# Two expert layers with the second product's weight held stationary and the rows turned back a block later

## The reference

```python
# layer 0: each row goes to one of 8 experts (arg max of the gate)
h = gelu(rows @ W1[e] + b1[e])          # 128 -> 512
f = h @ W2[e] + b2[e]                   # 512 -> 128
# layer 1: each row goes to its two best experts, each with a limited number of places
h = gelu(rows @ W1[e] + b1[e]);  ye = h @ W2[e] + b2[e]
f = ye[first] * w1 + ye[second] * w2
```

## Time and profile before

| | us |
|---|---|
| median of 3 runs | 1137.81 |
| the profiled execution, its time | 1137.35 |
| its span | 1135.5 |
| TensorE busy in the span | 1012.4 (89%) |
| expert stage, layer 0 (second products, first to last start) | 340.2 to 424.5 |
| expert stage, layer 1 | 945.7 to 1093.1 |

### The profile page before, as it was taken

One profiled execution on the slowest core, in us unless ns is written; L12 is line 12 of the kernel. 1 busy time (PEld: TensorE's weight loads), 2 busy tenths in 40 slices (PEclk: granted clock), 3 DMA queues, 4 the chain that ended last, 5 costly groups with the idle time before them and its releaser, 6 DMA issues.

```text
span 1135.5 us, 22426 instructions
## 1 busy us (share of the span) xinstructions
PE 1012.4 (89%) x6668; PEld 745.6 (66%) x6668; DVE 686.7 (60%) x2553; ACT 659.4 (58%) x1973; POOL 668.5 (59%) x821
## 2 busy tenths in 40 slices
PE   5798999999999999899999998998889978999950
PEld 2675566666668996566666665666568857989840
DVE  6737876776763336776776777867654353345326
ACT  4635667667755557667666666675554434544434
POOL 3425588788854555677676687887345422545443
PEclk9678999999999999999999999999999889999985
DMA  9200112202526742203302122032131044777745
GB/s 293 63 5 1 26 37 63 68 24 64 151 47 197 221 147 62 55 25 70 64 7 60 28 57 65 25 76 53 31 83 29 29 140 142 211 209 224 216 134 149
DMA packets 97385, 103.70 MB, mean 91 GB/s; under 512 B 10447, under 2 KB 85238, under 8 KB 97040
## 3 DMA queue, kind: packets, MB, share of 16 engines
q1 hardware_dynamic: 90256, 89.96, 30.2%
q0 software_dynamic: 7040, 12.66, 3.2%
HBM read 77.29 MB, written 25.28 MB: 90 GB/s over the span
## 4 chain that ended last, share of the span: by engine, by line
PE 55%; DVE 14%; issue 12%; ACT 8%; POOL 4%; DMA 3%; SPq 2%; another core or an unknown queue 1%; POOLq 0%; DVEq 0%; ACTq 0%
PE bank L1138 11%; PE bank L641 8%; PE bank L630 8%; PE bank L1167 7%; PE bank L1194 5%; PE bank L1182 4%; PE bank L1157 4%; DVE arena L1731 4%; PE bank L1219 3%; ACT arena L1479 3%; POOL arena L906 2%; DVE arena L1740 2%; ACT arena L1468 1%; PE bank L1071 1%; ACT XN L355 1%
## 5 line engine op out<-in xcount | busy, mean ns | idle before, releaser
L1479 ACT ACTIVATE arena<-arena 128x128 f32<-128x128 f32 (+1 forms) x512 | 226.9, 446 | 118.9 <-DVE arena L1731 118.4
L1731 DVE CUSTOM_DVE_ANT_0 arena<-bank,arena 128x128 f32<-128x128 f32 (+1 forms) x512 | 182.9, 413 | 141.1 <-PE bank L1167 134.8
L906 POOL TENSOR_TENSOR arena<-arena 128x512 f32<-128x512 f32 x128 | 132.7, 1042 | 164.4 <-ACT arena L1455 157.0
L1138 PE MATMUL bank<-arena 128*128 128x512 f32 x384 | 210.3, 637 | 15.5 <-ACT arena L1468 11.7
L1740 DVE COPY arena<-bank 128x384 f32<-128x384 f32 x256 | 130.3, 549 | 24.3 <-PE bank L1182 20.3
L604 POOL DMA_INDIRECT expert_out<-arena x78 | 77.0, 987 | 101.6 <-DVE arena L710 86.1
L921 POOL TENSOR_TENSOR arena<-arena 128x512 f32<-128x512 f32 x128 | 129.9, 1049 | 1.3
L1182 PEld LDWEIGHTS bank<-const,arena 128*128 128x128 f32 x768 | 91.7, 142 | 56.2 <-issue 56.0
L1455 ACT ACTIVATE arena<-bank 128x512 f32<-128x512 f32 x192 | 112.6, 587 | 26.9 <-PE bank L1138 26.7
L1167 PE MATMUL bank<-arena 64*128 64x128 f32 (+1 forms) x1024 | 120.0, 353 | 8.4 <-DVE arena L1731 5.5
L1194 PE MATMUL bank<-arena 128*64 128x256 f32 (+1 forms) x1024 | 111.8, 339 | 6.9 <-DVE arena L1740 6.3
(11 more groups left out here) (277 smaller groups left out, 1806.1 us busy)
## 6 DMA issues: line engine op xcount, KB each, us to landing
arena<-in_wp SPq DMA_DIRECT2D x39, 514.0 KB
arena<-recip_rows SPq DMA_DIRECT2D x30, 512.0 KB, 6.2
XN<-in_wp SPq DMA_DIRECT2D x23, 514.0 KB
arena<-expert_rows SPq DMA_DIRECT2D x62, 129.0 KB
arena<-expert_out SPq DMA_DIRECT2D x16, 256.0 KB, 5.4
arena<-in_b SPq DMA_DIRECT2D x62, 64.0 KB
expert_out<-fill SPq DMA_DIRECT2D x11, 338.6 KB, 7.6
expert_rows<-fill SPq DMA_DIRECT2D x1, 2967.0 KB, 22.5
```

The lines of the kernel that those rows point to most:

```text
L906: pool.tensor_tensor(sq[:, i % 2], r, r, ALU.mult).then_inc(S["sq_done"], 1)
L1138: mm = pe.matmul(RING[bnk][:, :], xa[:, p, t * P:(t + 1) * P], wqkv[:, 512 * k:512 * k + 512], start=True, stop=True)
L1479: ins = act.activation(w, w, ACT.Exp, bias=nm[:, p, 16 * t + h:16 * t + h + 1], scale=-1.0, accum_out=den[:, p, 16 * t + h:16 * t + h + 1])
L1731: ins = v.tensor_tensor_reduce(out=SPb[:, c % 2, 384 * k + P * t:384 * k + P * t + n], in0=SBANK[k][:, P * t:P * t + n], in1=alibi[:, h, N ...
```

## The change

The second product is turned round: W2's block is now the stationary operand and 256 columns of hidden values move, so its result has the 128 features on the partitions and the 256 rows as columns. The bias b2 is then one number per partition: it is loaded as a column of 128 partitions x 1, and ScalarE adds it as it takes the product out of PSUM (`biased`, into the new buffer `yT`). Layer 0's tanh and product work on `yT`. Since the rows must be sent as rows, TensorE transposes the two halves back (`back`), in the step of the next block between `up` and `down`, and VectorE copies them out (`rows_out`) ahead of its `evac_x`. GpSimd sends after that copy in both layers. SyncE reloads weights after `yT_evac`. After the last block each stream has one more `biased`, `back` and `rows_out`.

```diff
@@ ffn_sync
-                sp.dma_start(b2b[:, q], B2[bass.ds(e, 1)].to_broadcast([P, D])).then_inc(S[f"w_in{q}"], 16)
+                sp.dma_start(b2c[:, q:q + 1], B2[bass.ds(e, 1)].rearrange("e d -> d e")).then_inc(S[f"w_in{q}"], 16)
...
-                sp.wait_ge(S["ye_evac"], j + (base + 1))
+                sp.wait_ge(S["yT_evac"], j + (base + 1))
@@ ffn_send
-                pool.wait_ge(S["ye_evac" if layer else "y_ready"], j + (base + 1))
+                pool.wait_ge(S["ye_evac"], j + (base + 1))
@@ ffn_tensor, down and the new back
+                for c in range(FC):
+                    mm = pe.matmul(YB[p][:, 0:BLK], wb[:, q, DFF + c * D:DFF + (c + 1) * D], hT[:, p, c * BLK:(c + 1) * BLK],
+                                   start=(c == 0), stop=(c == FC - 1))
+                mm.then_inc(S["ye_full"], 1)
+
+            def back(j, q):
+
+                pe.wait_ge(S["yT_evac" if layer else "y_ready"], j + ((base if layer else 0) + 1))
                 for t in range(2):
-                    for c in range(FC):
-                        mm = pe.matmul(YB[p][:, t * D:(t + 1) * D], hT[:, p, c * BLK + t * P:c * BLK + (t + 1) * P],
-                                       wb[:, q, DFF + c * D:DFF + (c + 1) * D], start=(c == 0), stop=(c == FC - 1))
-                mm.then_inc(S["ye_full"], 1)
+                    mm = pe.transpose(YB[q % 2][:, BLK + t * D:BLK + (t + 1) * D], yT[:, q % 2, t * P:(t + 1) * P], ident)
+                mm.then_inc(S["y_turned"], 1)
@@ step
                     up(j + 1, (q + 1) % NBUF, i + (q + 1) // NBUF)
+                if not isinstance(j, int) or j:
+                    back(j - 1, (q + NBUF - 1) % NBUF)
                 down(j, q)
...
+            back(nblk - 1, (nblk - 1) % NBUF)
@@ ffn_scalar
-            def half_tanh(j, q, first=False):
-
-                act.wait_ge(S["ye_evac"], j + 1)
-                if not first:
-                    act.wait_ge(S["y_ready"], j - 1)
-                act.activation(th[:, q % 2, :], yb[:, q, :], ACT.Tanh, scale=0.5).then_inc(S["tanh_done"], 1)
+            def biased(j, q, first=False):
+                act.wait_ge(S["ye_full"], j + (base + 1))
+                if base or not first:
+                    act.wait_ge(S["y_turned"], j + (base - 1))
+                act.activation(yT[:, q % 2, :], bank[6 + q % 2][:, 0:BLK], ACT.Identity, bias=b2c[:, q:q + 1], scale=1.0)\
+                   .then_inc(S["yT_evac"], 1)
+                if not layer:
+
+                    act.wait_ge(S["yT_evac"], j + 1)
+                    act.activation(th[:, q % 2, :], yT[:, q % 2, :], ACT.Tanh, scale=0.5).then_inc(S["tanh_done"], 1)
 
             def both(j, q, i):
                 gelu(j, q, i)
-                half_tanh(j - 1, (q + NBUF - 1) % NBUF)
-
-            if layer:
-                quads(act, 0, nblk - 1, gelu)
-            else:
-                gelu(0, 0, 0)
-                for j in range(1, NBUF):
-                    gelu(j, j, 0)
-                    half_tanh(j - 1, j - 1, j < 3)
-                quads(act, NBUF, nblk - 1, both)
-                half_tanh(nblk - 1, (nblk - 1) % NBUF)
+                biased(j - 1, (q + NBUF - 1) % NBUF)
+
+            gelu(0, 0, 0)
+            for j in range(1, NBUF):
+                gelu(j, j, 0)
+                biased(j - 1, j - 1, j < 3)
+            quads(act, NBUF, nblk - 1, both)
+            biased(nblk - 1, (nblk - 1) % NBUF)
@@ ffn_vector
-            def add_b2(j, q, i):
-                v.wait_ge(S["ye_full"], j + (base + 1))
-                v.wait_ge(S[f"w_in{q}"], (i + (counts[q] + 1)) * 32)
-                v.tensor_tensor(yb[:, q, :].rearrange("p (t d) -> p t d", t=2),
-                                YB[q % 2][:, 0:2 * D].rearrange("p (t d) -> p t d", t=2),
-                                b2b[:, q].unsqueeze(1).to_broadcast([P, 2, D]), ALU.add).then_inc(S["ye_evac"], 1)
+            def rows_out(j, q):
+                v.wait_ge(S["y_turned"], j + (base + 1))
+                v.tensor_copy(yb[:, q, :], YB[q % 2][:, BLK:2 * BLK]).then_inc(S["ye_evac"], 1)
 
             def silu2(j, q):
 
                 v.wait_ge(S["tanh_done"], j + 1)
-                v.scalar_tensor_tensor(out=yb[:, q, :], in0=th[:, q % 2, :], scalar=1.0, in1=yb[:, q, :], op0=ALU.add,
+                v.scalar_tensor_tensor(out=yT[:, q % 2, :], in0=th[:, q % 2, :], scalar=1.0, in1=yT[:, q % 2, :], op0=ALU.add,
                                        op1=ALU.mult).then_inc(S["y_ready"], 1)
 
             def step(j, q, i, more=True):
-                if not layer and not (isinstance(j, int) and j == 0):
-                    silu2(j - 1, (q + NBUF - 1) % NBUF)
+                if not isinstance(j, int) or j:
+                    if not layer:
+                        silu2(j - 1, (q + NBUF - 1) % NBUF)
+                    rows_out(j - 1, (q + NBUF - 1) % NBUF)
                 if more:
                     evac_x(j + 2, (q + 2) % NBUF, i + (q + 2) // NBUF)
-                add_b2(j, q, i)
...
+            rows_out(nblk - 1, (nblk - 1) % NBUF)
```

More of the change, by code:

```diff
@@ L229, in block_kernel @@
         XNC = take(4 * ROW).rearrange("p (t d) -> p t d", d=ROW)
+        b2c1 = take(NBUF)
         O1, FC1, FFN1_AT = 10784, 24128, 14880
@@ L233, in block_kernel, with ffn_buffers @@
         GA = arena[:, 0:2 * NT * D].rearrange("p (k t n) -> p k t n", k=2, t=NT)
-        def ffn_buffers(wb, b2b, xb, hT, xbT, yb, idx):
-            return (wb.rearrange("p (i n) -> p i n", i=NBUF), b2b.rearrange("p (i n) -> p i n", i=NBUF),
+        def ffn_buffers(wb, yT, xb, hT, xbT, yb, idx):
+            return (wb.rearrange("p (i n) -> p i n", i=NBUF), yT.rearrange("p (i n) -> p i n", i=2),
                     xb.rearrange("p (i t n) -> p i t n", i=NBUF, t=2), hT.rearrange("p (i n) -> p i n", i=2),
@@ L252, in block_kernel @@
         FFNB = (FFN0, FFN1)
+        B2C = (spare[:, SIZES[1] + SIZES[2]:SIZES[1] + SIZES[2] + NBUF], b2c1)
         th = RA[:, SIZES[5] + SIZES[6]:SIZES[5] + SIZES[6] + 4 * D].rearrange("p (i n) -> p i n", i=2)
@@ L265, in block_kernel @@
             *[f"rows_in{q}" for q in range(NBUF)], *[f"w_in{q}" for q in range(NBUF)], "xT_full", "xT_evac", "h_full", "gelu_done",
-            "ye_full", "ye_evac", "send_seen", *[f"sent{q}" for q in range(NBUF)], "ids_ready", "filled", "x1_in0", "x1_in1", "tanh_done", "y_ready", "gated", "rows_known", "root_step",
+            "ye_full", "yT_evac", "y_turned", "ye_evac", "send_seen", *[f"sent{q}" for q in range(NBUF)], "ids_ready", "filled", "x1_in0", "x1_in1", "tanh_done", "y_ready", "gated", "rows_known", "root_step",
             *[f"y1_in{q}" for q in range(8)], "second_scaled", "first", "tables_ready", "turned1", "mixed", "silu_done", "mixed_in", "l1w_in", "l1w_ready", "z1_full", "z1_evac", "v1_full", "v1_evac", "s1_full", "ttr1_done", "exp1_done", "pt1_full",
@@ L553, in ffn_sync @@
             W, B2 = a[f"wp_{layer}"], a[f"b2_{layer}"]
-            wb, b2b, xb = FFNB[layer][0:3]
+            wb, _, xb = FFNB[layer][0:3]
+            b2c = B2C[layer]
             def load_rows(j, q):
@@ L617, in ffn_tensor @@
             XT, HB, YB = bank[0:2], bank[2:6], bank[6:8]
-            wb, _, xb, hT, xbT, _, _ = FFNB[layer]
+            wb, yT, xb, hT, xbT, _, _ = FFNB[layer]
             def turn(j, q, i):
@@ L660, in ffn_tensor @@
                 step(j, j % NBUF, j // NBUF, more=min(2, nblk - 1 - j))
+            back(nblk - 1, (nblk - 1) % NBUF)
         def ffn_scalar(act, layer, nblk, base, counts):
             HB = bank[2:6]
-            wb, hT, yb = FFNB[layer][0], FFNB[layer][3], FFNB[layer][5]
+            wb, yT, hT = FFNB[layer][0], FFNB[layer][1], FFNB[layer][3]
+            b2c = B2C[layer]
             def gelu(j, q, i):
@@ L673, in gelu @@
                 ins.then_inc(S["gelu_done"], 1)
-            def half_tanh(j, q, first=False):
-                act.wait_ge(S["ye_evac"], j + 1)
-                if not first:
-                    act.wait_ge(S["y_ready"], j - 1)
-                act.activation(th[:, q % 2, :], yb[:, q, :], ACT.Tanh, scale=0.5).then_inc(S["tanh_done"], 1)
+            def biased(j, q, first=False):
[7 more added lines that the diff above has]
+                    act.activation(th[:, q % 2, :], yT[:, q % 2, :], ACT.Tanh, scale=0.5).then_inc(S["tanh_done"], 1)
             def both(j, q, i):
                 gelu(j, q, i)
-                half_tanh(j - 1, (q + NBUF - 1) % NBUF)
-            if layer:
-                quads(act, 0, nblk - 1, gelu)
-            else:
-                gelu(0, 0, 0)
-                for j in range(1, NBUF):
-                    gelu(j, j, 0)
-                    half_tanh(j - 1, j - 1, j < 3)
-                quads(act, NBUF, nblk - 1, both)
-                half_tanh(nblk - 1, (nblk - 1) % NBUF)
+                biased(j - 1, (q + NBUF - 1) % NBUF)
[5 more added lines that the diff above has]
+            biased(nblk - 1, (nblk - 1) % NBUF)
         def ffn_vector(v, layer, nblk, base, counts, flat=NBUF, behind=None):
```

(2 more changed lines are left out.)

## The result

The changed kernel takes 1200.27 us as a median of 4 runs (1195.74 to 1205.55), the kernel before 1136.87 us beside it. The ratio is 1.0549 (95% interval 1.0519 to 1.0578), +63 us between the medians, where +38 were forecast; 1200.27 lies 1.3 us above the range. The profiled execution spans 1196.4 us, 60.9 more than before.

A forecast was written before the change was run, and what follows sets the result against it. TensorE bounded the kernel before; after the change, the send loop would set 4.45 us a block. Layer 0 +12.0, layer 1 +20.3 and stage ends +5.6 make +37.9 on 1137.35: 1175 us, range 1149 to 1199.

The forecast's parts named there:

- TensorE's floor: TensorE's own work per block in the expert stages: two products and two pairs of transposes, 3.90 us, 0.17 more than before.
- Rival A: Expert stages: weight loads set TensorE's pace, so fewer loads make the change faster, 1087 us; chance 5%.
- The loop of two steps through the send: Expert stages: up, back, rows_out, send, evac_x and up four blocks later close a loop of 8.90 us, 4.45 a block.
- The terms without d: Loop parts outside the send: waiting up 1.83, transposes 0.38, VectorE's copy 0.46, evac_x to up 0.63; 3.30 us.
- d: Time from VectorE's last instruction on a block's rows to evac_x four blocks later, covering two sends and landing; taken as 5.6 us.
- the lead: Time from the weight load's issue to the end of the second send's issue in the changed order, forecast 0.42 us.
- Rival C: A send completes only when the weight load does: release 4.66 us after weight issue, 5.3 a block, 1223 us; chance 10%.
- The ends: Last steps of both expert stages, where nothing covers back: +3.7 us in layer 0, +1.9 in layer 1, together +5.6.
- The covers: In mid-stage, biased, rows_out and the bias column hide behind other work; bounds 0 to -3 us in all.
- The table loads of layer 1: ScalarE's loop now enters with gelu loaded; eight loads took 10.3 us; between 0 and -5 us, taken as 0.
- Rival B: Landing stays as short as in layer 0, d = 4.71: 4.0 us a block, 1150 us; chance 22%.
- The clock: Sign of a wrong forecast: granted clock falling because TensorE idles in every step; not priced.

The follow-up runs named there:

- e1: Changed kernel with the row number copy taken out of evac_x and done two steps later, so evac_x waits for no send: 1135.23 us, ratio 1.0116 to the kernel before.
- e9: Kernel before with one wait added, so GpSimd sends a block only after the next block's second product: 1217.29 us, ratio 1.0693 to the kernel before.
- e3: Changed kernel with SyncE's weight reload waiting for rows_out instead of the bias add: ratio 1.0369 to the kernel before.
- e4: Changed kernel reloading only 257 of 1028 weight columns from block 4 on, so products use stale weights: ratio 1.0289 to the kernel before.
- e8: Changed kernel with back moved ahead of up in layer 1 only: ratio 1.0515 to the kernel before.
- e7: Changed kernel with a second 514 KB copied from DRAM to DRAM behind each weight load: ratio 1.0728 to the kernel before.
- e2: Changed kernel with b2 packed as a 1029th weight column instead of loaded by its own DMA: ratio 1.0576 to the kernel before.
- e11: Kernel before with only layer 1's first four gelus written out ahead of ScalarE's loop: 1123.08 us, ratio 0.9999 to the kernel before.

## Why the prediction was wrong

- **TensorE's floor, 3.90 us a block**: right to the hundredth in `e1`. Rival A falls with it: the 8 matmuls of 256 columns take 1.73 us, whatever the 6 weight loads saved; PEld fell from 0.91 to 0.70 of the stage while the kernel became slower.
- **The loop of two steps through the send**: right. It is in the chain, `e1` cuts it and gets the time back, `e9` builds it into the kernel before and loses as much. The terms without d (3.30) fit the changed kernel, `e3` and `e4` within 0.04 us a block.
- **d = 5.6 us**: this is the step that failed, by its landing. It measured 6.5. Over 56 blocks 0.9 / 2 us each is 25 us, and the forecast missed by 25. I had seen that the order of weight load and send sets the landing, and computed the lead as 0.42 us (0.27 measured); then I took the landing from the one block with such a lead, which had 2.6 where the locked pattern has 3.4. It was one block in 19, between others whose sends and loads kept another order. A single odd row was treated as the rule for a regime that the change makes permanent. The same trace held more: its landings have a median of 1.71 us at a lead of 3.19 in layer 0 (19 waits) and 2.40 at 2.29 in layer 1 (26 waits), so they grow as the lead shrinks, and the earlier trace rows stood off that trend.
- **Rival C**, the send completes only with the load, came nearer in this one respect, and its size was too large. In the changed kernel the release comes 408.70 - 404.98 = 3.72 us after the weight issue, not 4.66, and close behind the end of the traffic (share of the DMA engines in the next to last column):

```profile
407.50:408.00 0.50, 0.50 (x4) 0.28 (x2) 0.00 (x0) 0.12 (x2) 0.50 (x1) 1.00 0.90 253
408.00:408.50 0.50, 0.11 (x2) 0.00 (x0) 0.00 (x0) 0.47 (x2) 0.45 (x1) 1.00 0.54 149
408.50:409.00 0.50, 0.00 (x0) 0.00 (x0) 0.30 (x2) 0.35 (x1) 0.24 (x1) 1.00 0.04 11
```

  The release comes 3.7 us behind the weight issue at a lead of 0.3 us, 4.6 at 2.3 (`e3`), 4.85 at 3.3 (`e8`, layer 1), and 2.5 when a quarter is loaded (`e4`). C carried the 4.66 of the earlier trace rows, where the lead is 3.06 us, over to a lead of 0.42. The rule of the Trainium skill ("DMA: Bandwidth & Descriptors", Queues, rings and completion order), a semaphore written only behind the engine's earlier writes, is compatible with `e3` and `e4`, and with the 1.4 us of `e9`'s sends whose last load was issued 5.5 us before; `e7` could not test it, and plain sharing of the engines is not excluded. So the cause of the longer landing is open between these two; that the load and its place set it is shown.
- **The ends, +5.6**: measured +5.8. **The covers** of `biased`, `rows_out` and the bias column: right, all 0 on the path in mid-stage (TensorE never idle in `e1`, `e2` no faster). The table loads of layer 1 fell from nine to one with no gain alone (`e11`, 0.9999), so taking 0 was right.
- **Rival B** needed a landing of 1.6 us; in the changed order it does not come, and `e8` shows it only at a lead of 3.3 us. **The clock** did not fall: 1.00 in both windows. It did in `e9`, layer 1 (0.97).
- **The range** ended at d = 6.5 and a period of 4.9, which is where the time landed; 1.3 us were missing. I had the longest release of 7.05 us in the rows and gave it too little.

## What to carry to other kernels

When a result is handed on one step later, look for the ring whose slot it frees: the added latency is hidden until it closes a loop, and then each microsecond in the loop is paid over and over, divided by the steps that the loop spans. Price a landing by where it falls against the large loads in the new order, and where the rows of before hold only one such case, take the whole spread. A small thing that shares a ring with a slow one (here two row numbers with a send) deserves its own copy time; moving it two steps later made the loop vanish.

## What the runs showed of the hardware

The same two indirect sends (64 KB each, 128 rows of 512 B) land 3.4 us after their issue when a 514 KB load was issued 0.3 us ahead of the end of that issue, 2.3 at 2.3 us, 1.6 at 3.3 us, 1.4 when the last load was issued 5.5 us before and the next only behind it (`e9`), and 2.0 at 0.5 us when the load is a quarter as large. I had expected some dependence, not a factor of two so regular that 52 of 53 waits in two stages lie between 2.9 and 3.8 us. A second 514 KB, copied from DRAM to DRAM behind each load, did not lengthen the landing (3.48 us); its rate could not be read.
